# Softmax sums of two tiles at once, a copy moved to ScalarE, and output halves added on TensorE

## The reference

```
y  = layernorm(x)
q, k, v = 1x1 convolutions of y to 8 heads x 32
att  = softmax(q k^T / sqrt(32)) v          # in windows of 8x8 pixels, per head
loc  = conv3x3(v) + b_local
x1   = x + conv1x1(att + loc, w_out) + b_out
t    = layernorm(x1)
gate = top 2 of 8 experts of t @ Wg + bg, softmax over the two
out  = x1 + sum over the two of w_e * (gelu(t @ W1[e] + b1[e]) @ W2[e] + b2[e])
```

## Time and profile before

| | |
|---|---|
| time, median of 3 runs | 452.26 us (451.12 to 453.64) |
| the profiled execution | 449.9 us |
| its span, first to last instruction | 448.1 us |
| mean granted clock of PE | 0.978 of full speed |
| PE busy | 408.3 us (91%), 3921 matmuls |
| DVE busy | 364.7 us (81%), 1256 instructions |
| ACT busy | 334.7 us (75%), 889 instructions |
| POOL busy | 301.9 us (67%), 386 instructions |

### The profile page before, as it was taken

How to read it: one execution, slowest core, us unless ns; L and a number is a source line. 1 busy time by engine, 2 the same in 40 slices (tenths; PEclk the granted TensorE clock), 3 DMA queues, 4 the chain that set the end, 5 groups by cost and what they waited for, 6 DMA issues and landing times.

```text
span 448.1 us, 12477 instructions
## 1 busy us (share of the span) xinstructions
PE 408.3 (91%) x3921; PEld 276.2 (62%) x3921; DVE 364.7 (81%) x1256; ACT 334.7 (75%) x889; POOL 301.9 (67%) x386
## 2 busy tenths in 40 slices
PE   6898979899999899889889789688999999999995
PEld 6354434445454444445445345245999999999995
DVE  4678979978898998998998999889876788778632
ACT  2466688788887778778777765434998898898894
POOL 4233434775845888888887758566777777777775
PEclk8899989999999999999999899989999999999998
DMA  9916800000000000000000000013332222222210
GB/s 218 236 49 122 186 2 2 0 2 1 2 1 2 14 20 20 19 20 14 20 20 14 26 26 26 24 49 97 96 84 76 63 59 62 59 71 75 77 48 0
DMA packets 36168, 22.42 MB, mean 50 GB/s; under 512 B 13648, under 2 KB 33855, under 8 KB 36104
## 3 DMA queue, kind: packets, MB, share of 16 engines
q1 hardware_dynamic: 30264, 14.70, 14.8%
q0 software_dynamic: 4960, 6.45, 4.4%
q10 hardware_dynamic: 880, 0.48, 0.6%
HBM read 13.07 MB, written 9.27 MB: 50 GB/s over the span
## 4 chain that ended last, share of the span: by engine, by line
PE 54%; DVE 17%; issue 11%; ACT 10%; POOL 7%; DMA 2%; ACTq 0%; POOLq 0%; DVEq 0%
PE bank L1649 16%; PE bank L1635 8%; PE bank L1466 7%; PE bank L1389 5%; DVE mx L1159 3%; PE bank L1508 3%; PE bank L1495 3%; PE bank L1484 2%; DVE sm L1167 2%; POOL pn L641 2%; DVE gs L970 2%; ACT pt L789 2%; PE bank L1404 2%; POOL rows_hbm L617 1%; POOL out L656 1%
## 5 line engine op out<-in xcount | busy, mean ns | idle before, releaser
L641 POOL TENSOR_TENSOR pn<-pe_,rs 128x512 f32<-128x512 f32 x64 | 67.4, 1053 | 71.5 <-DVE rs L1170 69.5
L1466 PE MATMUL bank<-aa,bd 64*64 64x256 f32 x512 | 70.6, 392 | 11.5 <-ACT pt L789 8.3
L617 POOL DMA_INDIRECT rows_hbm<-rowb,posu x64 | 65.5, 1023 | 22.6 <-issue 15.6
L656 POOL DMA_INDIRECT out<-bt,zs x63 | 63.0, 1000 | 20.1 <-issue 14.6
L1469 PE MATMUL bank<-pt,bt 64*64 64x256 f32 x512 | 70.6, 393 | 0.0
L801 ACT ACTIVATE pe_<-sc 128x512 f32<-128x512 f32 x64 | 40.6, 634 | 39.0 <-DVE sc L1162 31.7
L1466 PEld LDWEIGHTS bank<-aa,bd 64*64 64x64 f32 x512 | 33.7, 134 | 45.6 <-issue 32.7
L1159 DVE TENSOR_REDUCE mx<-bank 128x8 f32<-128x512 f32 x64 | 43.8, 685 | 20.4 <-PE bank L1466 19.6
L761 ACT COPY zs<-bank 128x512 f32<-128x512 f32 x64 | 37.2, 580 | 12.3 <-PE bank L1469 12.2
L1162 DVE TENSOR_TENSOR sc<-bank,mx 128x512 f32<-128x512 f32 x64 | 44.3, 692 | 2.2
L1282 DVE SCALAR_TENSOR_TENSOR bt<-bank,zs 128x64 f32<-128x64 f32 x91 | 25.5, 280 | 24.6 <-PE bank L1649 23.2
(11 more groups left out here) (293 smaller groups left out, 1055.9 us busy)
## 6 DMA issues: line engine op xcount, KB each, us to landing
zs<-rows_hbm SPq DMA_DIRECT2D x91, 66.0 KB, 1.8
wloc<-in_L_conv_w_local SPq DMA_DIRECT2D x2, 1152.0 KB, 9.3
rows_hbm<-zrow SPq DMA_DIRECT2D x1, 1914.0 KB, 15.2
x_sb<-in_x SPq DMA_DIRECT2D x3, 512.0 KB, 10.8
wloc<-in_L_ffn_W SPq DMA_DIRECT2D x2, 512.0 KB, 6.7
rows_hbm<-rowb,posu POOLq DMA_INDIRECT x64
out<-bt,zs POOLq DMA_INDIRECT x63, 2.3
wrec<-in_w2b SPq DMA_DIRECT2D x1, 520.0 KB, 4.2
```

Source lines behind the costliest of these rows:

```text
L617: nc.gpsimd.indirect_dma_start(out=rows_hbm, out_offset=bass.IndirectOffsetOnAxis(ap=posu[:, t:t + 1], axis=0), in_=rowb[:, t], in_offset= ...
L641: nc.gpsimd.tensor_tensor(pn[:, v % 2, :].rearrange("p (h j) -> p h j", h=HEADS), pe_[:, v % 2], rs[:, v % 2].unsqueeze(2).broadcast_to([P ...
L656: nc.gpsimd.indirect_dma_start(out=out, out_offset=bass.IndirectOffsetOnAxis(ap=idx_j, axis=0), in_=ob[:, j % LANES], in_offset=None, boun ...
L1466: scored = nc.tensor.matmul(dots[v % 2][same, w * 2 * P:(w + 1) * 2 * P], xq[same, t % 2, 2 * v + w], aa[same, t % 2, :, j0:j0 + WT], star ...
```

## The change

The sum and reciprocal are taken for two tiles in one instruction, in slots 2 and 0, one slot later for the even tile. `pe_`, `sm` and `rs` get four buffers, so the exponential waits for the `pn` of four tiles back only. POOL still makes `pn` tile by tile, but waits for the pair's reciprocal. The copy of XT into `xq` goes from DVE (slot 1) to ACT (slot 2, ahead of the copies of the first two projections). YT becomes a matmul with `halves32`, two 64x64 identities on top of each other, so that it adds the two halves of the output as it turns them; DVE then needs one addition. `bt` is packed to 64 columns. PE waits at two places for constants that it was behind by other waits before.

```diff
+        halves32 = sb("halves32", [P, C])
-        bt = sb("bt", [P, 2, TG * 2, P])
+        bt = sb("bt", [P, 2, TG * 2, C])
-        pe_ = sb("pe_", [P, 2, HEADS, WT])
+        pe_ = sb("pe_", [P, TG, HEADS, WT])
-        sm = sb("sm", [P, 2, HEADS])
-        rs = sb("rs", [P, 2, HEADS])
+        sm = sb("sm", [P, TG, HEADS])
+        rs = sb("rs", [P, TG, HEADS])
...
+            for k in range(2):
+                rows_k = slice(k * C, (k + 1) * C)
+                pool.wait_ge(ident_ready, 7 + k)
+                nc.gpsimd.tensor_copy(halves32[rows_k], ident[rows_k, rows_k]).then_inc(ident_ready, 1)
...
-                        wait(pool, rs_ready, at(t, TG, v + 1))
+                        wait(pool, rs_ready, at(t, 2, v // 2 + 1))
                         wait(pool, pt_done, at(t, TG, v - 1))
-                        nc.gpsimd.tensor_tensor(pn[:, v % 2, :]..., pe_[:, v % 2], rs[:, v % 2]..., ALU.mult)
+                        nc.gpsimd.tensor_tensor(pn[:, v % 2, :]..., pe_[:, v], rs[:, v]..., ALU.mult)
...
                     if u == 2 and real(nxt):
+                        wait(act, xt_done, at(nxt, 1, 1))
+                        wait(act, dots_done, at(nxt, TG, -TG))
+                        nc.scalar.copy(xq[:, nxt % 2]..., turn[XT][:]...).then_inc(bd_ready, 1)
                         keys_out(nxt, 0)
                         keys_out(nxt, 1)
...
                         wait(act, sub_ready, at(t, TG, v + 1))
-                        wait(act, pn_ready, at(t, TG, v - 1))
-                        wait(act, sum_ready, at(t, TG, v - 1))
+                        wait(act, pn_ready, at(t, TG, v - 3))
...
-                    t, v = tile(g, u - 1)
-                    if real(t):
-                        wait(dve, exp_ready, at(t, TG, v + 1))
-                        nc.vector.reduce_sum(sm[:, v % 2], pe_[:, v % 2], axis=AX.X).then_inc(sum_ready, 1)
-                        wait(dve, sum_ready, at(t, TG, v + 1))
-                        wait(dve, pn_ready, at(t, TG, v - 1))
-                        nc.vector.reciprocal(rs[:, v % 2], sm[:, v % 2]).then_inc(rs_ready, 1)
-                    if u == 1 and real(nxt):
...
-                        nc.vector.tensor_copy(dst, src).then_inc(bd_ready, 1)
+                    t, v = tile(g, u - 2)
+                    if u % 2 == 0 and real(t):
+                        wait(dve, exp_ready, at(t, TG, v + 2))
+                        nc.vector.reduce_sum(sm[:, v:v + 2], pe_[:, v:v + 2], axis=AX.X).then_inc(sum_ready, 1)
+                        wait(dve, sum_ready, at(t, 2, v // 2 + 1))
+                        wait(dve, pn_ready, at(t, TG, v - 2))
+                        nc.vector.reciprocal(rs[:, v:v + 2], sm[:, v:v + 2]).then_inc(rs_ready, 1)
                     if u == 2 and real(prv2):
                         wait(dve, yt_done, at(prv2, 1, 1))
-                        nc.vector.tensor_tensor(tmp[:, b], src[:, :, 0], xs, ALU.add).then_inc(x1_ready, 1)
-                        wait(dve, x1_ready, at(prv2, 2, 1))
-                        nc.vector.tensor_tensor(xd, src[:, :, 1], tmp[:, b], ALU.add).then_inc(x1_ready, 1)
+                        nc.vector.tensor_tensor(x1[...], turn[YT][:, 0:TG * C]..., x_sb[...], ALU.add).then_inc(x1_ready, 2)
...
                         wait(pe, bd_ready, at(t, 1, 1))
+                        if is_step(t, 0):
+                            pe.wait_ge(wvo_ready, 1)
...
+                            if is_step(prv2, 0):
+                                pe.wait_ge(ident_ready, 9)
                             for k in range(TG):
-                                last = nc.tensor.transpose(turn[YT][:, k * P:(k + 1) * P], ys[:, prv2 % 2, k * P:(k + 1) * P], ident[:])
+                                last = nc.tensor.matmul(turn[YT][:, k * C:(k + 1) * C], ys[:, prv2 % 2, k * P:(k + 1) * P], halves32[:],
+                                                        start=True, stop=True)
```

More of the change, by code:

```diff
@@ L275, in program @@
         xq = bd[:, :, :, 0]
-        xw = bt[:, :, :, 0:C]
+        xw = bt[:]
         xr = zf[:, 0:SLOTS * ROW].rearrange("p (s r) -> p s r", s=SLOTS)
@@ L514, in _ @@
                 nc.gpsimd.tensor_copy(both16[rows_k], ident16[rows_k, rows_k].unsqueeze(1).broadcast_to([C, 2, C])).then_inc(ident_ready, 1)
-            pool.wait_ge(ident_ready, 7)
+            for k in range(2):
+                rows_k = slice(k * C, (k + 1) * C)
+                pool.wait_ge(ident_ready, 7 + k)
+                nc.gpsimd.tensor_copy(halves32[rows_k], ident[rows_k, rows_k]).then_inc(ident_ready, 1)
+            pool.wait_ge(ident_ready, 9)
             nc.gpsimd.memset(xsp[:], 0.0).then_inc(zeroed, 1)
@@ L638, in body @@
                             normalise(nn, u)
-                        wait(pool, rs_ready, at(t, TG, v + 1))
+                        wait(pool, rs_ready, at(t, 2, v // 2 + 1))
                         wait(pool, pt_done, at(t, TG, v - 1))
-                        nc.gpsimd.tensor_tensor(pn[:, v % 2, :].rearrange("p (h j) -> p h j", h=HEADS), pe_[:, v % 2],
-                                                rs[:, v % 2].unsqueeze(2).broadcast_to([P, HEADS, WT]), ALU.mult).then_inc(pn_ready, 1)
+                        nc.gpsimd.tensor_tensor(pn[:, v % 2, :].rearrange("p (h j) -> p h j", h=HEADS), pe_[:, v],
+                                                rs[:, v].unsqueeze(2).broadcast_to([P, HEADS, WT]), ALU.mult).then_inc(pn_ready, 1)
             for u in range(1, TG):
@@ L793, in body @@
                     if u == 2 and real(nxt):
+                        wait(act, xt_done, at(nxt, 1, 1))
+                        wait(act, dots_done, at(nxt, TG, -TG))
+                        nc.scalar.copy(xq[:, nxt % 2].rearrange("p (t n) (y c) -> p t y n c", n=2, y=WSZ),
+                                       turn[XT][:].rearrange("p (t y n c) -> p t y n c", t=TG, y=WSZ, n=2)).then_inc(bd_ready, 1)
                         keys_out(nxt, 0)
@@ L798, in body @@
                         wait(act, sub_ready, at(t, TG, v + 1))
-                        wait(act, pn_ready, at(t, TG, v - 1))
-                        wait(act, sum_ready, at(t, TG, v - 1))
-                        nc.scalar.activation(pe_[:, v % 2], sc[:, v % 2], ACT.Exp,
+                        wait(act, pn_ready, at(t, TG, v - 3))
+                        nc.scalar.activation(pe_[:, v], sc[:, v % 2], ACT.Exp,
                                              scale=SCALE / XS / XS).then_inc(exp_ready, 1)
@@ L1179, in body @@
+                    if u % 2 == 0 and real(t):
[4 more added lines that the diff above has]
+                        nc.vector.reciprocal(rs[:, v:v + 2], sm[:, v:v + 2]).then_inc(rs_ready, 1)
                     if u == 2 and real(prv2):
-                        src = turn[YT][:].rearrange("p (t k c) -> p t k c", t=TG, k=2)
@@ L1182, in body @@
-                        b = prv2 % 2
                         wait(dve, yt_done, at(prv2, 1, 1))
-                        xs = x_sb[:, bass.ds(idx(prv2, TG), TG), :]
-                        xd = x1[:, bass.ds(idx(prv2, TG), TG), :]
-                        nc.vector.tensor_tensor(tmp[:, b], src[:, :, 0], xs, ALU.add).then_inc(x1_ready, 1)
-                        wait(dve, x1_ready, at(prv2, 2, 1))
-                        nc.vector.tensor_tensor(xd, src[:, :, 1], tmp[:, b], ALU.add).then_inc(x1_ready, 1)
+                        nc.vector.tensor_tensor(x1[:, bass.ds(idx(prv2, TG), TG), :], turn[YT][:, 0:TG * C].rearrange("p (t c) -> p t c", t=TG),
+                                                x_sb[:, bass.ds(idx(prv2, TG), TG), :], ALU.add).then_inc(x1_ready, 2)
```

## The result

The changed kernel takes 496.3 us (491.6 to 497.0, 4 runs) against 451.7 us for the kernel before in the same runs: a ratio of 1.098 (95% interval 1.093 to 1.103), +44.6 us. The forecast was 459 us with a range of 446 to 466. The direction was right, the size six times too small.

What follows compares the result with a forecast made beforehand. PE was taken to bound plain groups, with DVE and POOL as full in routed ones. Terms 1.5 + 0 + 4.3 + 1.7 - 0.4 = +7.1 us on 449.9 gave 457.0, plus 2.4 to the median 459.4: 459, range 446 to 466.

Steps and rivals of the forecast that it cites:

- DVE sheds 1.65 us a group: On DVE: the moved copy, paired sums and dropped add save 1.65 us a group, 26 us over 16 groups.
- Plain group, nothing lost: In groups without routing, pn of tile 2 comes 0.1 us late, with nothing gained and nothing lost.
- The ramp and groups 2 to 7: At the start: the late first tile 2 costs +1.5 us (between 0 and 2.7); groups 2 to 7 cost 0.
- Routed pair +1.4: Two groups with one batch routed: +1.4 us a pair (bounds -2.2 and +3), +4.3 us for three pairs.
- The freed operation: In routed pairs on DVE: the 8-column operation of 2.34 us ends 1.04 us earlier, without pn beside it.
- End +1.7, less 0.4: At the last sums: the last pn ends at 279.0 us instead of 277.3, +1.7, less 0.4 for the last add.
- The sum's length: On DVE: a sum of 1024 columns takes 1.19 us; from sum start to pn start 1.5 us instead of 1.0.
- YT's wait for the copy stays covered: On PE: YT's bank is asked for after two projections, so the wait for the moved copy costs nothing.
- PE's price of the adding matmuls, 0: On PE, output halves: matmul 275 ns, transpose 273 ns, so 0 (bounds -0.2 and +0.2 us a group).
- The rival that named a dearer matmul: Output halves on PE: each matmul 0.1 us dearer, 64 of them give +6 us, mostly under cover; no chance given.
- POOL becomes the bound: Rival: POOL, idle then in bursts, decides once pn(2) is over 1 us late at every pair; +13.8 us, 466; chance 0.13.
- The faster rival: DVE sets the pace of routed groups; a pair comes down to 30.1 us; 444.7 us, half of that 448.5; chance 0.27.

Runs made afterwards that it cites:

- pn_last: The kernel before with the paired sums alone, both pn of a pair placed behind POOL's other work of both slots: 461.0 us, ratio 1.022.
- pair01: The kernel before with only tiles 0 and 1 sharing a sum; tiles 2 and 3 keep their own: 464.5 us, ratio 1.028.
- halves: The kernel before with only the adding matmuls for the output halves and the single DVE addition: 456.4 us, ratio 1.011.

## Why the prediction failed, by its steps

*DVE sheds 1.65 us a group.* Right, to the sum of 26 us, and of no use here: DVE waited for PE afterwards.

*Plain group, nothing lost: wrong, and the main failure.* It placed the next group's subtraction at its old time, found pn(2) 0.1 us late, and stopped at pn. The same rule that it applied to pn(3) in the routed pair (all that is queued behind the waiting pn(2)) it didn't apply to hl and the routing norm, though it listed both as work between the two pn. It never asked who reads them: PE's transposes of the next tokens, which stand right behind tile 2's, and ACT's halves, ahead of the key copies and `pt`. The plain group of the rows above lost 2.5 us by it and by the two other parts (the groups before it 1.1 to 4.3 each); with the queue in order, in pn_last, the same group takes 14.76 us and loses 0.4. The ramp and groups 2 to 7, taken at +1.5, lost 24.1. The same omission is in "Tile 0 has PE's four projections as cover" (13.5 us by pair01).

*Routed pair +1.4:* measured +4.0, +8.2 and +8.4, all beyond the bound of 3. The freed operation was right: the 8-column subtraction takes 165 ns in the changed kernel, not 980 (group of line 979). But it was credited against a path that had moved to POOL's queue.

*End +1.7, less 0.4: wrong.* From the last copy on nothing was lost (203.2 us against 203.4).

*The sum's length.* 0.5 us later was in the terms, but as part of a wait compared once, not as time on the path 32 times.

*YT's wait for the copy stays covered: wrong.* The copy follows `pt` on ACT, which needs the transposes just before the projections; 0.6 + 0.6 us against 0.9 us of projections. PE waited 9.1 us in all. I had the durations and didn't add them. The copy alone cost 8.0, where the sum had about 1.5 (0.5 in three pairs).

*PE's price of the adding matmuls, 0: wrong.* The row for 128x64 f32 shows 275 ns, but its count is two records a matmul (728 for 91 blocks of four), and one for a transpose. From start to next start the four matmuls took 0.83 to 0.94 us against 0.43. The rival that named a dearer matmul had 0.1 us each, which is what halves shows, and gave +6 "mostly under cover"; it was +5.2 of 6.4 and not under cover.

*The cause between the rivals.* "POOL becomes the bound" had POOL idle and late in bursts, at 466. Its condition, pn(2) over 1 us late, was met at once, but it isn't POOL's rate: POOL is busy 60% in the changed kernel. It is the order of its queue, as pn_last shows. That 466 would have been nearer than 459 is no merit of its cause. The faster rival's pair of 30.1 us was reached by no run that pairs the sums; the nearest is 31.0 us, with both orders mended, and there the relief of DVE isn't shown to be the cause.

*The clock, which had no term.* PE's granted clock was 0.946 over the profiled run of the changed kernel against 0.978 before. The four executions of the changed kernel run from 497.0 us at 0.946 to 491.6 us at 0.973. At 0.973, close to the 0.978 of the kernel before, it is still 41.7 us behind that execution (449.9 us). So the spread in the clock goes with some 5 us, and the rest was there at nearly the old clock; how much the fall from 0.978 to 0.973 and its place in the run cost stays open.

## What to carry to other kernels

An instruction that waits longer delays everything behind it in its engine's queue, so the cost of a new wait is read from the readers of all those instructions, slot by slot, and not from the waiting instruction's own reader. Work that needs nothing late belongs ahead of the wait: here that order was worth 28 us with no operation made faster. And before a batched operation is placed, look for the earliest point at which its inputs exist; the same paired sums cost 8.5% behind the subtraction, and at the head of the slot, with the queue in order, nothing.

## What the runs showed of the hardware

Groups of line 1575 in the kernel before and here in the changed one:

```profile
L1575 PE MATMUL bank<-halves,ys 128*128 128x64 f32 x128 | 18.1, 287 | 10.0 <-ACT bd L802 9.1 <-ACT ys L833 0.9
L1575 PEld LDWEIGHTS bank<-halves,ys 128*128 128x128 f32 x128 | 16.4, 200 | 17.3 <-ACT bd L802 15.5 <-issue 1.7
```

An f32 transpose of 128 columns cost PE 0.11 us (0.43 / 4, from start to next start, in the kernel before), an f32 matmul of half the columns with the same weights 0.21 us (0.83 / 4, in halves), in two records each. The mean of a record, 273 and 287 ns, doesn't show it; the count does. The Trainium skill has both halves of this: "TensorE: Matmul & The Clock Gate" (Terms) says that the transpose mode is 4 times faster for FP32, and "FP8 and Floating Point Precision" (TensorE Precision Notes) that a true FP32 product takes four passes. With half the columns that makes twice the time, an estimate from the two pages; the traces agree, with 1.9 times (0.83 against 0.43 us). The weight loads are dearer too, 200 against 140 ns.

Small DVE operations with two SBUF inputs can be held beside POOL's work. Of the eight 8-column subtractions of the kernel before, three took 2.33 to 2.34 us (mean of all 980 ns); each began 0.1 us before POOL's `xn` and ended within 0.05 us of the end of the pn two instructions behind it. Not every meeting does it: the one at 256.20 us began 0.02 us behind a pn and took 0.17 us. In the changed kernel no pn runs beside them, and the mean is 165 ns. In the kernel with the copy alone it is 163 ns, while the operation one line up rose from 315 to 970: there that one began together with `xn` and was held to the end of pn.
